# Another order of work at the beginning of a transformer block on one core

## The reference

```
x = x + 0.5 * ffn(layernorm(x), k0, k1, k2, s0, s1, s2)
x = x + attn(layernorm(x), w_q, w_k, w_v, w_o, b_o)
x = x + 0.5 * ffn(layernorm(x), k0, k1, k2, s0, s1, s2)
def ffn(x, ...):
    h = concatenate([x, -x], axis=-1)
    h = s0 * h @ where(k0, 1, -1);  h = relu(h) * 2
    h = s1 * h @ where(k1, 1, -1);  h = relu(h) * 2
    return s2 * h @ where(k2, 1, -1)
def attn(x, ...):
    q, k, v = x @ w_q.T, x @ w_k.T, x @ w_v.T      # 16 heads of 16
    p = softmax(where(causal, -1e9, q k.T / 4))
    return (p v) @ w_o.T + b_o
```

## Time and profile before

| | us |
|---|---|
| median of 3 runs | 1689.33 |
| lowest and highest | 1683.36, 1690.95 |
| profiled execution | 1687.42 |
| its span | 1685.7 |
| one chunk of phase A in the steady state | 53.63 |

### The profile page before, as it was taken

One profiled execution on the slowest core, in us unless ns is written; L12 is line 12 of the kernel. 1 busy time (PEld: TensorE's weight loads), 2 busy tenths in 40 slices (PEclk: granted clock), 3 DMA queues, 4 the chain that ended last, 5 costly groups with the idle time before them and its releaser, 6 DMA issues.

```text
span 1685.7 us, 40071 instructions
## 1 busy us (share of the span) xinstructions
PE 1610.8 (96%) x14224; PEld 731.9 (43%) x14224; DVE 1158.1 (69%) x1746; ACT 948.2 (56%) x1703; POOL 160.1 (9%) x320
## 2 busy tenths in 40 slices
PE   6899999999989999898999999999997899999998
PEld 3455555555533333333333333333332455555554
DVE  6545543454589888787887878878886556666632
ACT  2223223232279999797997989889997222222211
POOL 5200000000011111111111111111110000000000
PEclk9999999999999999999999999999999899999999
DMA  5011013110131112220122202222213111113000
GB/s 172 0 51 50 0 50 87 50 36 14 49 104 50 37 51 65 59 65 26 49 65 59 65 30 51 59 60 63 59 44 102 51 51 50 50 50 110 15 12 13
DMA packets 115790, 89.42 MB, mean 53 GB/s; under 512 B 76080, under 2 KB 95152, under 8 KB 115632
## 3 DMA queue, kind: packets, MB, share of 16 engines
q1 hardware_dynamic: 115632, 87.20, 18.0%
HBM read 49.15 MB, written 37.75 MB: 52 GB/s over the span
## 4 chain that ended last, share of the span: by engine, by line
PE 87%; DVE 3%; issue 3%; ACT 2%; DMA 2%; SPq 2%; DVEq 0%; ACTq 0%
PE ffn_mm L400 26%; PE ffn_mm L1201 16%; PE ffn_mm L1222 13%; PE ffn_mm L388 7%; PE ffn_acc L416 7%; PE ffn_acc L568 5%; PE ffn_tr L568 5%; PE ffn_mm L667 3%; PE ffn_acc L679 2%; ACT probs L1161 2%; PE ffn_acc L488 1%; PE ffn_tr L375 1%; PE ffn_tr L573 1%; DVE qk L1282 1%; DMA qk<-ctx_scr 1%
## 5 line engine op out<-in xcount | busy, mean ns | idle before, releaser
L1161 ACT ACTIVATE probs<-ffn_mm,exp_scale 128x512 f32<-128x512 f32 (+3 forms) x1280 | 705.5, 641 | 96.4 <-PE ffn_mm L1201 90.7
L1201 PE MATMUL ffn_mm<-qk 66*32 66x512 f16 (+7 forms) x5120 | 413.5, 359 | 25.2 <-issue 19.9
L588 DVE TENSOR_REDUCE m_part<-ffn_acc 128x2 f32<-128x1024 f32 (+1 forms) x314 | 351.2, 1119 | 76.4 <-PE ffn_acc L568 44.1
L400 PE MATMUL ffn_mm<-ffn_h1h,w 128*128 128x512 f16 x1024 | 389.4, 380 | 7.5 <-DVE ffn_h2l L453 7.5
L400 PE MATMUL ffn_mm<-ffn_h1l,w 128*128 128x512 f16 x1024 | 389.2, 380 | 0.0
L588 DVE TENSOR_REDUCE m_part<-ffn_tr 128x2 f32<-128x1024 f32 (+3 forms) x326 | 328.0, 1006 | 28.6 <-PE ffn_tr L573 15.4
L1222 PE MATMUL ffn_mm<-probs,v 128*32 128x512 f32 (+3 forms) x2560 | 307.7, 538 | 2.3
L446 ACT ACTIVATE ffn_h2h<-ffn_mm 128x512 f16<-128x512 f32 x128 | 76.2, 598 | 309.2 <-PE ffn_mm L400 294.5
L1201 PEld LDWEIGHTS ffn_mm<-qk 66*32 66x32 f16 (+1 forms) x5120 | 131.5, 94 | 252.3 <-ACT probs L1161 136.0
L453 DVE SCALAR_TENSOR_TENSOR ffn_h2l<-ffn_mm,ffn_h2h 128x512 f16<-128x512 f32 x128 | 86.3, 688 | 188.5 <-ACT ffn_h2h L446 188.5
L1114 POOL TENSOR_SCALAR_AFFINE_SELECT probs<-probs 128x256 f32<-128x256 f32 (+1 forms) x256 | 108.0, 422 | 734.8 <-ACT probs L1161 734.6
(11 more groups left out here) (99 smaller groups left out, 1104.9 us busy)
## 6 DMA issues: line engine op xcount, KB each, us to landing
qk<-qk_scr SPq DMA_DIRECT2D x256, 64.0 KB, 2.6
ctx_scr<-ctx_out SPq DMA_DIRECT2D x64, 256.0 KB, 2.8
qk<-ctx_scr SPq DMA_DIRECT2D x64, 256.0 KB
v_scr<-v_pad SPq DMA_DIRECT2D x32, 256.0 KB, 2.9
v<-v_scr SPq DMA_DIRECT2D x16, 512.0 KB, 4.6
x_res<-L_attn_x SPq DMA_DIRECT2D x8, 512.0 KB, 3.8
qk_scr<-qk_hi SPq DMA_DIRECT2D x32, 128.0 KB, 1.8
qk_scr<-qk_lo SPq DMA_DIRECT2D x32, 128.0 KB, 1.8
```

The lines of the kernel that those rows point to most:

```text
L400: ins = nc.tensor.matmul(f.mm[:, m % 4, :], w1[:, kt, m * P:(m + 1) * P], part[:, kt, :], start=(kt == 0 and part is f.h1h), stop=(kt == H ...
L588: nc.vector.tensor_reduce(m_part[u][:, t, :, r], s_ps[slot][:, :, 0:w], AX.X, ALU.max).then_inc(sb.s_done, 1)
L1161: nc.scalar.activation(probs[:, g % P_SLOTS, j, c0:CH], st_ps[bank(k)][:, c0:CH], ACT.Exp, scale=exp_scale[:, 0:1]).then_inc(se.exp_done, 1)
L1201: ins = nc.tensor.matmul(st_ps[bank(k)][c:c + 32, c0:CH], k_part(u, h, rows, slice(kb * P + c, kb * P + c + 32)), q_part(u, h, rows, slice ...
```

## The change

Six edits, all ahead of the end of chunk 0.

1. SP issues the three scalars right behind x of chunk 0, ahead of k0.
2. DVE finishes the layer norm of chunk 0 before it touches the scalars.
3. `w_diff` and `w0` are made in two halves of columns. DVE makes both of the left one; of the right one DVE makes the difference, behind `ffn_xl`, and ACT the product, behind `ffn_xh`. PE waits for the left half at tile 0 of the first layer and for the right at tile 4. The two halves of `w1` are waited for one by one, at matmuls of tile 0 of the second layer.
4. The 16 transposes of the attention weights move on PE from the place ahead of the first layer into the second layer of chunk 0, between tiles 2 and 3, into `ffn_tr` and `ffn_acc`. The copies on ACT move too.
5. ACT waits for the two scales before chunk 1, no longer before chunk 0.
6. POOL clears the rows of `qk` only once DVE has written both scales.

```
@@ SP
                 sp.dma_start(x_res[:, 0:TPC, :], x_chunks[0]).then_inc(se.x_in, 16)
-                sp.dma_start(k0_u8[:, :, :], k0.rearrange("(t p) f -> p t f", p=P)).then_inc(se.k0_in, 16)
                 for n, s in enumerate((s0, s1, s2)):
                     sp.dma_start(s_in[:, n:n + 1], ...).then_inc(se.s_in, 16)
+                sp.dma_start(k0_u8[:, :, :], k0.rearrange("(t p) f -> p t f", p=P)).then_inc(se.k0_in, 16)
@@ POOL
                 pool.wait_ge(se.wamax, 1)
+                pool.wait_ge(se.wscale, 2)
@@ DVE
                 dve_ln_stats(ln1, 0)
+                dve_ln_finish(ln1, 0, f.sem.t_ps)
                 dve.wait_ge(se.s_in, 48)
...
-                dve_ln_finish(ln1, 0, f.sem.t_ps)
-
+                left, right = slice(0, HID // 2), slice(HID // 2, HID)
                 dve.wait_ge(se.k0_in, 16)
-                nc.vector.tensor_tensor(w_diff[:, :, :], k0_u8[:, 0:DT, :], k0_u8[:, DT:, :], ALU.subtract).then_inc(se.w0d, 1)
+                nc.vector.tensor_tensor(w_diff[:, :, left], k0_u8[:, 0:DT, left], k0_u8[:, DT:, left], ALU.subtract).then_inc(se.w0d, 1)
...
-                nc.vector.tensor_scalar(w0[:, :, :], w_diff[:, :, :], w0_mul[:, 0:1], None, ALU.mult).then_inc(se.w0, 1)
+                nc.vector.tensor_scalar(w0[:, :, left], w_diff[:, :, left], w0_mul[:, 0:1], None, ALU.mult).then_inc(se.w0, 1)
                 dve_x(f, 0)
+                nc.vector.tensor_tensor(w_diff[:, :, right], k0_u8[:, 0:DT, right], k0_u8[:, DT:, right], ALU.subtract).then_inc(se.w0d, 1)
@@ ACT
                 act_x(f, 0)
-                for n in range(4):
-                    act.wait_ge(se.wt_ps, n + 1)
-                    nc.scalar.activation(w_t[:, n, :, :], f.mm[:, n, :]..., ACT.Copy).then_inc(se.wt, 1)
+                act.wait_ge(se.w0d, 2)
+                act.wait_ge(se.sprep, 1)
+                nc.scalar.activation(w0[:, :, HID // 2:], w_diff[:, :, HID // 2:], ACT.Copy, scale=w0_mul[:, 0:1]).then_inc(se.w0_right, 1)
                 act_hidden(f, 0, range(HT), 0)
                 act_ln_sqrt(ln1, 1)
-                act.wait_ge(se.wscale, 2)
-                act.wait_ge(se.vones, 1)
...
                     act_hidden(f, c, range(0, 3), 1)
-                    if not first:
+                    if first:
+                        act_wt()
+                    else:
                         act_x2(c - 1, proj_in)
...
                 act_ln_sqrt(ln1, 2)
+                act.wait_ge(se.wscale, 2)
+                act.wait_ge(se.vones, 1)
                 chunk(1)
@@ PE
                 pe_t1(0, first=True)
-                pe.wait_ge(se.w_in, 64)
...
-                pe.wait_ge(se.w0, 1)
+                def pe_wt():
+                    pe.wait_ge(se.w_in, 64)
+                    for n in range(4):
+                        ...  # 4 transposes each, into (f.tr, f.acc)[n // 2][:, n % 2, ...]
...
-                    pe_l1(f, c, range(0, 3), l1_free(c, first))
-                    if not first:
+                    pe_l1(f, c, range(0, 3), l1_free(c, first), rows=w1_rows if first else None)
+                    if first:
+                        pe_wt()
+                    else:
                         pe_t2(c - 1)
...
-                pe.wait_ge(se.w1, 2)
                 chunk(0, first=True)
```

More of the change, by code:

```diff
@@ L130, in __init__ @@
         self.w0 = new("w0")
+        self.w0_right = new("w0_right")
         self.w1 = new("w1")
@@ L390, in pe_l0, with pe_l1 @@
                 ins.then_inc(f.sem.l0_ps, 1)
-        def pe_l1(f, c, ms, free, fill=None):
+        def pe_l1(f, c, ms, free, fill=None, rows=None):
             for m in ms:
@@ L398, in pe_l1 @@
                         wait(nc.tensor, f.sem.l0_lo, c * HT + kt + 1)
+                        if rows:
+                            rows(kt)
                     for part in (f.h1h, f.h1l):
@@ L917, in _, with act_wt @@
                 act_x(f, 0)
-                for n in range(4):
-                    act.wait_ge(se.wt_ps, n + 1)
-                    nc.scalar.activation(w_t[:, n, :, :], f.mm[:, n, :].rearrange("p (t d) -> p t d", t=DT),
-                                         ACT.Copy).then_inc(se.wt, 1)
+                act.wait_ge(se.w0d, 2)
+                act.wait_ge(se.sprep, 1)
+                nc.scalar.activation(w0[:, :, HID // 2:], w_diff[:, :, HID // 2:], ACT.Copy, scale=w0_mul[:, 0:1]).then_inc(se.w0_right, 1)
                 act_hidden(f, 0, range(HT), 0)
                 act_ln_sqrt(ln1, 1)
-                act.wait_ge(se.wscale, 2)
-                act.wait_ge(se.vones, 1)
+                def act_wt():
+                    for n in range(4):
+                        act.wait_ge(se.wt_ps, n + 1)
+                        nc.scalar.activation(w_t[:, n, :, :], (f.tr, f.acc)[n // 2][:, n % 2, :].rearrange("p (t d) -> p t d", t=DT),
+                                             ACT.Copy).then_inc(se.wt, 1)
                 def chunk(c, first=False):
                     act_hidden(f, c, range(0, 3), 1)
-                    if not first:
+                    if first:
+                        act_wt()
+                    else:
                         act_x2(c - 1, proj_in)
@@ L964, in _, with w1_rows @@
                 pe_t1(0, first=True)
-                pe.wait_ge(se.w_in, 64)
[L966 to L971, removed]
-                pe.wait_ge(se.w0, 1)
+                def pe_wt():
+                    pe.wait_ge(se.w_in, 64)
+                    for n in range(4):
+                        for jt in range(DT):
+                            for it in range(DT):
+                                ins = nc.tensor.transpose((f.tr, f.acc)[n // 2][:, n % 2, it * D + jt * P:it * D + (jt + 1) * P],
+                                                          w_in[:, n, jt, it * P:(it + 1) * P], ident[:, :])
+                        ins.then_inc(se.wt_ps, 1)
                 def l0_free(c):
+                    first = isinstance(c, int) and c == 0
                     def free(m):
-                        if m < 4 and isinstance(c, int) and c == 0:
-                            wait(pe, se.wt, m + 1)
-                        elif m < 4:
+                        if first and m == 0:
+                            wait(pe, se.w0, 1)
+                        if first and m == HT // 2:
+                            wait(pe, se.w0_right, 1)
+                        if m >= 4:
+                            wait(pe, f.sem.l0_lo, c * HT + m - 3)
+                        elif not first:
                             wait(pe, f.sem.l1_lo, (c - 1) * HT + 5 + m)
-                        else:
-                            wait(pe, f.sem.l0_lo, c * HT + m - 3)
-                    return free
+                    return free
+                def w1_rows(kt):
+                    if kt % (HT // 2) == 0:
+                        wait(pe, se.w1, kt // (HT // 2) + 1)
                 def l1_free(c, first):
@@ L997, in free @@
                             wait(pe, se.w2, 1)
+                            wait(pe, se.wt, 4)
                         else:
@@ L1016, in chunk @@
                     pe_l1(f, c, range(4, 6), l1_free(c, first))
+                    if first:
+                        wait(pe, se.wt, 2)
                     pe_t1(c + 1, first=first)
```

## The result

| | before | changed |
|---|---|---|
| median of 16 runs each, us | 1690.34 | 1676.81 |
| lowest and highest | 1682.69, 1694.57 | 1672.6, 1680.29 |
| span of the profiled execution | 1685.7 | 1675.0 |
| start of the third layer of chunk 0 in it | 66.97 | 53.91 |

The ratio is 0.9925, 95% interval 0.9912 to 0.9937: 12.7 us or 0.75% faster. The forecast was 1674.7, range 1667.5 to 1681.

What follows compares the result with a forecast made beforehand. PE, with 87% of the chain of waits, bounds the kernel; time comes off only where it stands still or runs slow. The terms' -13.65 us gave 1673.8 or 1675.7 from two bases, middle 1674.7, range 1667.5 to 1681.

Steps and rivals of the forecast that it cites:

- The sum: Up to chunk 0's third layer, all terms together: -6.10 + 0.35 - 9.64 + 1.74 = -13.65 us.
- Step 1: Start of chunk 0 on DVE: layer norm no longer waits for the scalars, removing 2.97 us.
- The rival on k0: Start of chunk 0: scalars issued ahead delay k0, PE starts 3.09 us late, time 1677.8; chance 0.09.
- Step 2: Weights ahead of `ffn_xl`: only half made there, first layer starts at 14.04, gain 6.10 us; right half costs nothing.
- Step 3: First layer of chunk 0 on PE: ten matmuls at the low rate, 1.95 us lost where it was 1.60, cost 0.35.
- Step 4: Second layer of chunk 0: with clears behind the scales PE's stall goes whole, 7.69 idle plus 1.95 low rate, gain 9.64 us.
- Step 5: Second layer of chunk 0: the 16 transposes now stand on PE's path, eight taking 0.87, cost 1.74 us.
- The low clock: Rival, first layer on PE: clock stays low throughout, cost 5.31 in place of 0.35, time 1679.7; chance 0.07.
- The gain is not carried: Rival, phase B: its gaps or loads grow by what came off ahead, time 1688; chance 0.04.
- The slower rival: Phase A's loop: a gap at each of five returns, 5.95 us each, +29.8, time 1704.5; chance 0.04.

Runs made afterwards that it cites:

- e8: Changed kernel plus 40 identity transposes on PE ahead of chunk 0's transposes and 20 behind them; third layer at 51.20, median 1667.74 us.
- e11: Changed kernel plus nine identity transposes on PE between x's transposes and the first layer, none ahead; third layer at 56.23, median 1680.39 us.
- e10: e8 with the scalars issued behind k0 again; third layer at 53.61, median 1673.34 us.
- e9: Changed kernel with POOL's `w1` begun only once DVE has made the right half's difference; third layer at 53.41, median 1676.87 us.
- e12: e8 with k0 ahead of the scalars and POOL's `w1` behind the right half's difference; third layer at 50.72, median 1667.7 us.

## Why the prediction was right, point by point

**The sum.** Predicted -13.65 at the third layer, measured -13.06; measured for the program 12.7 by ratio and 13.5 by medians. The forecast of 1674.7 is a middle of two bases, the profiled execution and the median of three runs. From the median of 16 runs, 1690.34, the same sum gives 1676.7, 0.1 under the measured 1676.81; with single executions 8 to 12 us apart, so close a hit is luck.

**Step 1** held: `ln_xn` was out 2.9 earlier, the first layer started at 14.12 (predicted 14.04). But edit 1 was idle: with the layer norm ahead, the order of the DMAs does nothing (first layer at 14.17 without it). The rival on k0 did not come, though e8 shows how near it was: DVE waited 0.46 for k0 there.

**Step 2** held at its end and failed inside. The left half cost 0.49, well under the 1.39 taken. The right half's difference was put at 1.15, at worst 2.29; it took 3.10 there and 2.8 to 4.2 elsewhere. It was covered in the changed kernel, because twelve matmuls at the low rate brought PE to tile 4 late, and not in edits 1 to 4 alone (0.9), e11 (2.50) and e10 (2.99). So the "nothing" of this term came out by luck: its reason, that a bank is wanted only four tiles later, does not hold at the high rate when the difference is held up. The Trainium skill (GPSIMD Engine Reference, 1. Specifications) says that POOL shares its SBUF interfaces with VectorE, with contention for VectorE instructions with two SBUF inputs. The trace agrees with it, 3.10 beside `w1` against 1.22 in e9. The bound I took from one row was no bound, since `w_diff` had begun 0.16 ahead of POOL there; and the 4.14 that I halved was no rate, but mostly a wait: the product, begun at 14.71, ended at 18.85, 0.55 behind the first half of `w1`.

**Step 3** was a little small: twelve matmuls, not ten; 5.06 us for what takes 2.59, so 2.47 lost where 1.95 was put. That is 0.52 of the 0.59 between the sum and the measurement, and the first layer's start 0.08 late is the rest. It is also no property of the order alone: with 24 transposes ahead, eight were low before, nine with edit 5 alone, three with the transposes back at the start, and none with edit 6 alone.

**Step 4** was right in size and cause, and it is the largest part of the change: edit 6, one line, is worth 9.7 at the third layer without the luck of its execution, where 9.64 was put. Its ratio, 0.9903 to 0.9956, cannot be told from the changed kernel's. Edit 5 gives nothing beside it. Only the picture was too narrow: it had one clear for each `ln_xn`, but the clears also held `w_lim` and `w_pow`, for 3.2 together. The scales were out at 33.1 (predicted 33.9 at the latest), and the low parts beside the clears took 0.65 to 0.69 each, no more than elsewhere.

**Step 5** was exact: 0.87 and 0.87. Undone, edit 4 costs 1.8 net, because the first layer then waits for the attention weights.

**The rivals.** The low clock lasted for twelve of the 32 matmuls. "The gain is not carried": from the third layer on it took 1618.7 before and 1621.1 after in the profiled pair; the same stretch took 1619.2 to 1629.0 in the other kernels without much new code, so 2.4 is scatter, and the medians carry the gain. The slower rival had its mechanism in the wrong place: phase A has no gap at its loop's return after either, but phase B's gaps do change with what stands ahead (below).

## What to carry to other kernels

A long wait in the list may be parallel to the one that decides: ask whose output the bottleneck asks for next, and follow that engine's order. Housekeeping on POOL belongs where DVE runs nothing that it holds up, and one wait placed for that can be worth more than a reordered start. When a start is made faster, look at what a slow part of it was hiding, here a race between two engines that only the low clock covered.

## What the runs showed of the hardware

**POOL and DVE.** An instruction of the kinds below waits for the end of the one that POOL is running, and so its own size hardly matters. With a clear running, every `TENSOR_SCALAR` of the layer norm and the first two of the scales (one tensor input, SBUF to SBUF) waited: `ln_xn`, 256 elements, took 1.83 in place of 0.35, and `w_lim`, 2 elements, 1.84 in place of 0.16, beside clears of 1.80 to 1.94. The product for `w0` took 4.14 begun after `w1`, 0.75 begun before it. The difference, two uint8 inputs, took 1.22 begun first and 2.83 to 4.23 begun after `w1`, and then always ended 1.07 behind the first half of `w1`. It works the other way too: that first half took 5.76 before, where the difference had begun 0.16 ahead of it, and 3.76 in e9 and e12, with none of these beside it. Not held beside the clears were `RECIPROCAL`, `TENSOR_TENSOR` in float32 (0.16 to 0.18 each) and the statistics, and neither beside `w1` nor beside the clears those with an input in PSUM: 1.29 for two of `ffn_xl`, 0.69 for a low part.

**The gaps at phase B's loop.** PE's waits named "issue" (in total, times, longest) of the changed kernel, of e8 and of e12:

```profile
PE ffn_mm L1227 <- issue: 20.6, 5, 4.6
```

```profile
PE ffn_mm L1234 <- issue: 15.9, 5, 3.5
```

```profile
PE ffn_mm L1235 <- issue: 16.0, 5, 3.4
```

In the three kernels with 60 more transposes ahead, the five gaps make 15.9 to 16.2 us; in the eleven others 18.8 to 21.7. So some 4 us of what e8 and e12 win come from there and not from the clock at the start. That the position of PE's code decides it is my guess; no run moved the code alone.
